# VectorE adds three of the last four pair sums of the softmax stage, and GpSimd does the small steps of the second norm's variances

## The chip, the cores and the metric

The kernel runs on one core of a Trainium2 chip. The metric is the device time of one execution in microseconds; the median of three runs is shown, with the lowest and the highest. The profile is of one more execution.

## What is computed

The input has four batches of 2048 tokens with 256 features. A block with two halves is applied to each batch. The first half is a layer norm with modulation, then attention by random features (16 heads, 64 features each). The second half is a second norm with modulation, a third norm, and softmax attention in which the tokens of expert e use only the first 256 / 2^e features.

```python
h = _layernorm(x, axis=-1) * (1 + ca) + sa
x = x + ga * _L0_attn_ref(h, ...)          # random features
h = _layernorm(x, axis=-1) * (1 + cb) + sb
x = x + gb * _L0_ffn_ref(h, ...)           # per token: xn = _layernorm(h), q, k, v by expert,
                                           # softmax(q k^T * scale) v over all 2048 tokens
```

A layer norm needs the mean and the variance of each token over its 256 features, and (variance + epsilon) to the power of -1/2.

## The kernel before, in words

Each engine has its own program, written out by hand, and semaphores tie them together. The loop over the four batches is written out too. A batch has three stages.

**First stage.** 16 tiles of 128 tokens: norm, projections, random features, sums over the keys. GpSimd prepares the first two tiles of the next batch in `begin` (two reciprocal roots L486, two normalised tiles `XH` L502), and `low_h` (L493) makes the low part `HTR` that TensorE's projection (L1424) needs.

**Middle stage.** The 2048 tokens are four slots of 512, and each slot has two halves (s, h) of two tiles. In the order of VectorE's program: `merged` (MT, L1147) multiplies numerators and reciprocals, TensorE projects (L1579), `residual` (L1154) adds, `statistics_of_x` takes the statistics of X (BATCH_NORM_STATS L1004, BATCH_NORM_AGGREGATE L1008 into MV, which holds mean and variance) and writes VE = variance + epsilon (L1014), GpSimd raises VE to -1/2 (RSTD, L572, in `deviations`), `modulated` (L1165, L1169) writes Hh, `statistics_of_h` takes the statistics of Hh and writes NEGM = -mean (L1013) and VE (L1014), and GpSimd writes RSTD (L577) and NMR = NEGM * RSTD (L579) in `deviations_again`. ScalarE then normalises (`centred`, L781, and `normal`, L793), TensorE makes queries and keys (L1608), ScalarE and VectorE write them as a high and a low part (QKS, L810 and L1179, `high_part` and `low_part`), and SyncE stores them and loads them back in the layout of the scores (the scratch tensors k_scr and q_scr, the tiles KOP and QOP). The interleaving of these steps is a list of calls in each engine's program. On GpSimd the list is `deviations(0, 0)`, `deviations(0, 1)`, `deviations_again(0, 0)` and so on.

**Softmax stage.** 64 steps called slots, in eight groups of eight (this slot is not the slot of 512 tokens). In each, TensorE makes four score tiles (L1705), ScalarE takes their exponentials into PR (L901), and TensorE multiplies by the values (L1717). The four tiles of a slot are added in pairs (the pair sum, TS0 and TS1) so that TensorE can form the denominators of two slots at once (L1730). GpSimd makes the pair sums (L631), except those of `VECTOR_SUMS`, slots 61 and 63 of 0 to 63, which VectorE makes (`pair_sum`, L1289). Beside this VectorE takes the maxima of scores of later units (L1111). In the last batches of slots GpSimd runs `begin(b + 1)` behind the sum of slot 60, and VectorE has begun the next batch just before its sum of slot 61. Behind slot 63 the order on TensorE is: the denominators of slots 62 and 63, the next batch's projection (L1424), its values (L1432), and the last output (L1785, L1787).

Of the kernel before, what the change touches and what calls it, by code (L numbers as in the profile page):

```python
# [7 lines left out]
ALU = mybir.AluOpType  # L8
# [12 lines left out]
NORM_EPS = 1e-5  # L21
# [24 lines left out]
def adaln_block(nc, x, Wq, Wk, Wv, Wo, bo, proj, norm_w, norm_b, q_w, q_b, k_w, k_b, v_w, v_b, o_w, o_b,  # L46
# [58 lines left out]
    with ExitStack() as ctx:  # L105
# [107 lines left out]
        def out_ps(e):  # L213
# [8 lines left out]
                   ve2 rs3 rstd2 ve3 nmr3 h2 x2 x2T xn_sb qp q_hi q_lo scr0 scr1 scr2 vp v2_sb vb_ok obm  # L222
# [85 lines left out]
        VECTOR_SUMS = (SLOTS - 3, SLOTS - 1)  # L308
# [163 lines left out]
        def _(pool):  # L472
            g = nc.gpsimd
# [68 lines left out]
            def batch(b):  # L542
# [26 lines left out]
                def deviations(s, h):  # L569
                    cols, n = halves(s, h), 2 * (NC * b + s) + h + 1  # L570
                    wait_all(pool, (S["ve2"], n))
                    g.tensor_tensor(RSTD[:, cols], VE[:, cols], minus_half[:, cols], ALU.pow).then_inc(S["rstd2"], 1)  # L572

                def deviations_again(s, h):
                    cols, n = halves(s, h), 2 * (NC * b + s) + h + 1
                    wait_all(pool, (S["ve3"], 2 * n))
                    g.tensor_tensor(RSTD[:, cols], VE[:, cols], minus_half[:, cols], ALU.pow).then_inc(S["rs3"], 1)  # L577
                    wait_all(pool, (S["rs3"], n))
                    g.tensor_tensor(NMR[:, cols], NEGM[:, cols], RSTD[:, cols], ALU.mult).then_inc(S["nmr3"], 1)  # L579
# [345 lines left out]
        def _(dve):  # L925
# [75 lines left out]
            def statistics(tiles, srcs, signal, negated=False):  # L1001
# [5 lines left out]
                for t in tiles:  # L1007
                    v.bn_aggr(MV[:, t], STAT[:, t]).then_inc(S["dve_own"], 1)  # L1008
                    own.n += 1
                dve.wait_ge(S["dve_own"], own.base + own.n)  # L1010
                sl = slice(tiles[0], tiles[-1] + 1)
                if negated:
                    v.tensor_scalar(NEGM[:, sl], MV[:, sl, 0], -1.0, None, ALU.mult).then_inc(S[signal], 1)  # L1013
                v.tensor_scalar(VE[:, sl], MV[:, sl, 1], NORM_EPS, None, ALU.add).then_inc(S[signal], 1)  # L1014
# [50 lines left out]
            def batch(b):  # L1065
# [106 lines left out]
                def statistics_of_h(s, h):  # L1172
                    dve.wait_ge(S["h2"], TPC * (NC * b + s) + 2 * h + 2)
                    statistics(halves(s, h), [Hh[:, t] for t in halves(s, h)], "ve3", negated=True)
# [72 lines left out]
                for m in range(SLOTS // 2):  # L1247
# [23 lines left out]
                    if 2 * m == SLOTS - 2:  # L1271
                        pair_sum(b, SLOTS - 1)
# [567 lines left out]
```

## Time and profile before

| what | value |
|---|---|
| median of three runs | 1766.48 us (1762.68 to 1766.83) |
| the profiled execution, its own time | 1768.27 us |
| its span, first to last instruction | 1766.5 us |
| mean granted TensorE clock | 0.974 |
| TensorE busy | 1678.5 us, 95% |
| VectorE busy | 1385.5 us, 78% |
| GpSimd busy | 1126.5 us, 64% |
| ScalarE busy | 1085.4 us, 61% |

The first batch ends at about 472 us of the span (the last addition into X, L1305, at 470.97), and each later one is some 431 us long, of which the middle stage has about 80 (165 to 245 us in the first batch) and the softmax stage about 220. In the timelines the columns are start, duration, engine, line, operation, output and input, how many are merged, and in brackets how long the engine had been idle and who released it. A busy TensorE is modelled, and the other engines' durations overlap a little between neighbours. Granted clock 1.00 is TensorE's upper level, 0.50 its lower.

### The profile page before, as it was taken

To read this page: it belongs to the slowest core of one execution; us is meant where nothing else is said; L and a number is where in the kernel's file an instruction comes from. 1 tells how busy PE (TensorE), PEld (TensorE's weight loads), DVE (VectorE), ACT (ScalarE), POOL (GpSimd) and SP (SyncE) were. 2 spreads that over 40 slices of the span, in tenths; PEclk is the share of its full clock that TensorE was granted. 3 is DMA by queue.
4 is the path that set the end of the run, shared out by engine and by line. 5 is a ranking of instruction groups with operands and counts; after the bars stand their busy time and mean duration, and the time that the engine had idled before them with its cause. 6 is when DMAs were issued, how large, how long until landed. Compare 5 with 4: busy or idle time off the path is not lost.

```text
span 1766.5 us, 32009 instructions
## 1 busy us (share of the span) xinstructions
PE 1678.5 (95%) x11538; PEld 970.8 (55%) x11538; DVE 1385.5 (78%) x2629; ACT 1085.4 (61%) x2066; POOL 1126.5 (64%) x1058
## 2 busy tenths in 40 slices
PE   6999989999999989999999998999999999899998
PEld 4776544444577554444467755444437765444443
DVE  5987978787688788787678878877858878787783
ACT  1885536566688553565668844466667875356665
POOL 2784358767678344867767734686686862477675
PEclk8999989999999998999999999999999999899999
DMA  6000360010200045001110005400120001520101
GB/s 188 2 1 1 103 188 15 19 46 25 73 2 1 1 152 143 10 19 46 58 40 2 2 16 174 106 19 10 46 72 25 2 1 58 179 61 18 39 17 48
DMA packets 56077, 89.57 MB, mean 51 GB/s; under 512 B 13288, under 2 KB 31976, under 8 KB 53100
## 3 DMA queue, kind: packets, MB, share of 16 engines
q1 hardware_dynamic: 54768, 87.45, 17.0%
q8 instruction: 93, 1.52, 0.4%
q14 instruction: 64, 0.52, 0.1%
q10 hardware_dynamic: 1152, 0.07, 0.0%
HBM read 49.29 MB, written 35.72 MB: 48 GB/s over the span
## 4 chain that ended last, share of the span: by engine, by line
PE 68%; DVE 16%; ACT 9%; DMA 2%; issue 2%; SPq 1%; POOL 1%; ACTq 0%; DVEq 0%; POOLq 0%
PE PS L1530 13%; PE PS L1705 12%; PE PS L1717 12%; PE PS L1730 6%; PE PS L1424 5%; DVE MXP L1111 4%; PE PS L1449 4%; PE PS L1432 3%; PE PS L1459 3%; ACT HT L670 2%; ACT HTR L673 2%; DVE STAT L1004 2%; ACT PR L901 2%; DVE QKS L1179 1%; ACT PHIQ L711 1%
## 5 line engine op out<-in xcount | busy, mean ns | idle before, releaser
L631 POOL TENSOR_TENSOR TS<-PR 128x1024 f32<-128x1024 f32 (+1 forms) x248 | 551.6, 2238 | 259.8 <-ACT PR L901 195.4
L1111 DVE TENSOR_REDUCE MXP<-PS 128x1 f32<-128x512 f32 x960 | 589.0, 681 | 145.9 <-PE PS L1530 145.2
L901 ACT ACTIVATE PR<-PS 128x512 f32<-128x512 f32 x960 | 487.6, 622 | 285.3 <-PE PS L1705 261.8
L1530 PE MATMUL PS<-KOP,QOP 96*128 96x512 f32 x960 | 406.8, 437 | 10.2 <-DVE MXP L1111 3.5
L1705 PE MATMUL PS<-QOP,KOP 97*128 97x512 f32 x960 | 376.5, 424 | 3.5 <-ACT QOP L888 3.1
L1530 PEld LDWEIGHTS PS<-KOP,QOP 96*128 96x128 f32 x960 | 186.2, 195 | 169.3 <-issue 90.4
L1705 PEld LDWEIGHTS PS<-QOP,KOP 97*128 97x128 f32 x960 | 180.3, 190 | 143.7 <-ACT PR L901 110.2
L1717 PE MATMUL PS<-PR,V 128*32 128x512 f32 x1920 | 255.1, 597 | 0.5
L1730 PE MATMUL PS<-TS,ones 128*32 128x512 f32 x960 | 136.0, 604 | 6.7 <-DVE TS L1289 6.7
L1717 PEld LDWEIGHTS PS<-PR,V 128*32 128x32 f32 x1920 | 62.2, 110 | 140.6 <-issue 98.4
L549 POOL TENSOR_SCALAR PK<-XSK 128x1024 f32<-128x1024 f32 x64 | 67.2, 1050 | 100.3 <-ACT XSK L733 100.3
L1459 PE MATMUL PS<-PB,QKT 64*128 64x256 f32 x1536 | 125.4, 296 | 1.0 <-DVE VE L998 1.0
L1459 PEld LDWEIGHTS PS<-PB,QKT 64*128 64x128 f32 x1536 | 99.2, 186 | 36.8 <-issue 24.4
L1424 PE MATMUL PS<-W1T,HTR 128*128 128x512 f32 x384 | 108.5, 419 | 3.7 <-POOL HTR L493 3.7
L509 POOL TENSOR_TENSOR SQ<-SQ 128x256 f32<-128x256 f32 (+2 forms) x192 | 95.9, 500 | 20.8 <-ACT SQ L690 6.0
L1051 DVE TENSOR_REDUCE MXQ<-PS 128x16 f32<-128x1024 f32 x64 | 78.4, 1224 | 21.8 <-PE PS L1459 21.2
L1449 PE MATMUL PS<-ident,XSQ 128*128 128x128 f32 x512 | 84.5, 292 | 9.8 <-ACT PHIQ L711 9.8
L502 POOL TENSOR_SCALAR XH<-X,MV,RSTD 128x256 f32<-128x256 f32 x64 | 78.7, 1229 | 11.0 <-POOL RSTD L486 10.4
L1061 DVE TENSOR_TENSOR XSK<-PS,MXK 128x1024 f32<-128x1024 f32 x64 | 78.4, 1225 | 7.1 <-DVE MXK L1057 0.9
L1051 DVE TENSOR_REDUCE MXK<-PS 128x16 f32<-128x1024 f32 x64 | 78.4, 1225 | 6.6 <-PE PS L1459 2.0
L711 ACT ACTIVATE PHIQ<-PS 128x512 f32<-128x512 f32 x128 | 76.5, 598 | 10.7 <-PE PS L1449 10.7
L1424 PEld LDWEIGHTS PS<-W1T,HTR 128*128 128x128 f32 x384 | 68.6, 192 | 25.1 <-POOL HTR L493 6.5
(157 smaller groups left out, 2524.1 us busy)
## 6 DMA issues: line engine op xcount, KB each, us to landing
KOP<-k_scr SPq DMA_DIRECT2D x84, 256.0 KB, 5.7
k_scr<-QKS SPq DMA_DIRECT2D x64, 256.0 KB, 2.9
QOP<-q_scr SPq DMA_DIRECT2D x180, 64.0 KB, 2.0
q_scr<-QKS SPq DMA_DIRECT2D x40, 256.0 KB, 3.0
X<-in_L_attn_x_dram SPq DMA_DIRECT2D x16, 512.0 KB, 3.9
out_dram<-X SPq DMA_DIRECT2D x12, 512.0 KB, 3.0
QOP<-MXT SPq DMA_DIRECT2D x224, 0.5 KB
KOP<-QKS SPq DMA_DIRECT2D x36, 64.0 KB, 2.0
```

What stands on the lines that cost most here:

```text
L509: g.tensor_tensor(sq[:, :, 0:w], sq[:, :, 0:w], sq[:, :, w:2 * w], ALU.add).then_inc(S["n2_half"], 1)
L631: g.tensor_tensor(sums(k)[:, 0:len(stage)], pair[:, :, 0], pair[:, :, 1], ALU.add).then_inc(S["psum_t"], 1)
L901: a.activation(PR[:, k % 2, w, q], bank(score_bank(p, n, w, q)), ACT.Exp).then_inc(S["ex"], 1)
L1051: return mark(v.tensor_reduce(mx[:], heads(src), AX.X, ALU.max))
L1111: v.tensor_reduce(MXP[:, u % 2, i, kc:kc + 1], bank(max_bank(p)), AX.X, ALU.max).then_inc(S["am_rd"], 1)
L1424: last = mm(bank(4), HTR[:, x_, k], W1T[:, w_, k], start=m == 0 and k == 0, stop=m == len(PARTS) - 1 and k == KD - 1)
L1449: last = tr(bank(at_bank)[:, q * P:(q + 1) * P], XSQ[:, t % 2, (half * 4 + q) * P:(half * 4 + q + 1) * P], ident[:])
L1459: last = mm(bank(base + r)[:, 2 * P * j:2 * P * (j + 1)], QKT[rows, x_, 2 * j + o], PB[rows, w_, j, 2 * P * r:2 * P * (r + 1)], start=m == ...
L1530: mm(bank(max_bank(p)), QOP[0:96, u % QS6, i * P:(i + 1) * P], KOP[0:96, h % KS6, kc * CH:(kc + 1) * CH], start=True, stop=True).then_inc( ...
L1705: mm(bank(score_bank(p, n, w, q)), KOP[:, units[u][0] % KS6, kt * P:(kt + 1) * P], QOP[:, u % QS6], start=True, stop=True).then_inc(S["sc_ ...
L1717: last = mm(PS[r:r + DH, 6, :], V2[:, 2 * n + q, h * DH:(h + 1) * DH], PR[:, k % 2, w, q], start=n == 0, stop=n == STEPS - 1, tile_positio ...
L1730: last = mm(PS[r:r + DH, 7, :], ones[:], sums(2 * m + q)[:, w], start=n == 0, stop=n == STEPS - 2, tile_position=(0, r))
```

## The change

Three edits. The sum of slot 62 joins `VECTOR_SUMS`, and VectorE makes it just before that of slot 63. `statistics` on VectorE ends with the aggregation, which signals by itself (one signal per tile, so the waits count two per half). VE and NEGM are now written by GpSimd, with three new semaphores between GpSimd's own steps.

```diff
-        VECTOR_SUMS = (SLOTS - 3, SLOTS - 1)
+        VECTOR_SUMS = (SLOTS - 3, SLOTS - 2, SLOTS - 1)
...
                 def deviations(s, h):
                     cols, n = halves(s, h), 2 * (NC * b + s) + h + 1
-                    wait_all(pool, (S["ve2"], n))
+                    wait_all(pool, (S["ve2"], 2 * n))
+                    g.tensor_scalar(VE[:, cols], MV[:, cols, 1], NORM_EPS, None, ALU.add).then_inc(S["ve2_e"], 1)
+                    wait_all(pool, (S["ve2_e"], n))
                     g.tensor_tensor(RSTD[:, cols], VE[:, cols], minus_half[:, cols], ALU.pow).then_inc(S["rstd2"], 1)
 
                 def deviations_again(s, h):
                     cols, n = halves(s, h), 2 * (NC * b + s) + h + 1
                     wait_all(pool, (S["ve3"], 2 * n))
+                    g.tensor_scalar(VE[:, cols], MV[:, cols, 1], NORM_EPS, None, ALU.add).then_inc(S["ve3_e"], 1)
+                    g.tensor_scalar(NEGM[:, cols], MV[:, cols, 0], -1.0, None, ALU.mult).then_inc(S["negm"], 1)
+                    wait_all(pool, (S["ve3_e"], n))
                     g.tensor_tensor(RSTD[:, cols], VE[:, cols], minus_half[:, cols], ALU.pow).then_inc(S["rs3"], 1)
-                    wait_all(pool, (S["rs3"], n))
+                    wait_all(pool, (S["rs3"], n), (S["negm"], n))
                     g.tensor_tensor(NMR[:, cols], NEGM[:, cols], RSTD[:, cols], ALU.mult).then_inc(S["nmr3"], 1)
...
-            def statistics(tiles, srcs, signal, negated=False):
+            def statistics(tiles, srcs, signal):
 
                 for t, src in zip(tiles, srcs):
                     v.bn_stats(STAT[:, t], src).then_inc(S["dve_own"], 1)
                     own.n += 1
                 wait_all(dve, (S["dve_own"], own.base + own.n))
                 for t in tiles:
-                    v.bn_aggr(MV[:, t], STAT[:, t]).then_inc(S["dve_own"], 1)
-                    own.n += 1
-                dve.wait_ge(S["dve_own"], own.base + own.n)
-                sl = slice(tiles[0], tiles[-1] + 1)
-                if negated:
-                    v.tensor_scalar(NEGM[:, sl], MV[:, sl, 0], -1.0, None, ALU.mult).then_inc(S[signal], 1)
-                v.tensor_scalar(VE[:, sl], MV[:, sl, 1], NORM_EPS, None, ALU.add).then_inc(S[signal], 1)
+                    v.bn_aggr(MV[:, t], STAT[:, t]).then_inc(S[signal], 1)
...
                         pair_sum(b, SLOTS - 3)
                     if 2 * m == SLOTS - 2:
+                        pair_sum(b, SLOTS - 2)
                         pair_sum(b, SLOTS - 1)
```

How the lists of instructions move is shown at three places. GpSimd, start of the middle stage of a batch, before (`PK`, `BOG` belong to the first stage):

```order
L540 TENSOR_TENSOR X<-X,BOG 128x256 x8
L572 TENSOR_TENSOR RSTD<-VE,minus_half 128x2 x2
L577 TENSOR_TENSOR RSTD<-VE,minus_half 128x2
L579 TENSOR_TENSOR NMR<-NEGM,RSTD 128x2
L577 TENSOR_TENSOR RSTD<-VE,minus_half 128x2
```

The same place in the changed program:

```order
L572 TENSOR_SCALAR VE<-MV 128x2 [waits ve2]
L574 TENSOR_TENSOR RSTD<-VE,minus_half 128x2 [waits ve2_e]
L572 TENSOR_SCALAR VE<-MV 128x2 [waits ve2]
L574 TENSOR_TENSOR RSTD<-VE,minus_half 128x2 [waits ve2_e]
L579 TENSOR_SCALAR VE<-MV 128x2 [waits ve3]
L580 TENSOR_SCALAR NEGM<-MV 128x2
L582 TENSOR_TENSOR RSTD<-VE,minus_half 128x2 [waits ve3_e]
L584 TENSOR_TENSOR NMR<-NEGM,RSTD 128x2 [waits negm,rs3]
```

GpSimd has one more step ahead of each first root and two ahead of each second one, and the root waits for GpSimd's own result.

VectorE at the same half as slot (1, 0), before:

```order
L1004 BN_STATS STAT<-X 128x6 x2
L1008 BN_AGGR MV<-STAT 128x2 x2
L1014 TENSOR_SCALAR VE<-MV 128x2
L1135 TENSOR_SCALAR R<-PS 128x4x8 x2
L1139 RECIPROCAL R<-R 128x64
L1165 SCALAR_TENSOR_TENSOR Hh<-X,MV,MODB 128x256 x2
```

and now, where the step on VE is gone and nothing else moved:

```order
L1009 BN_STATS STAT<-X 128x6 x2
L1013 BN_AGGR MV<-STAT 128x2 x2
L1134 TENSOR_SCALAR R<-PS 128x4x8 x2
L1138 RECIPROCAL R<-R 128x64
L1164 SCALAR_TENSOR_TENSOR Hh<-X,MV,MODB 128x256 x2
```

GpSimd at the end of a batch's softmax stage (the sum of slot 60, `begin` of the next batch, the sum of slot 62, `low_h`), before:

```order
L631 TENSOR_TENSOR TS0<-PR 128x1024
L486 TENSOR_TENSOR RSTD1<-VE1,minus_half 128x1
L502 TENSOR_SCALAR XH<-X,MV1,RSTD1 128x256
L486 TENSOR_TENSOR RSTD1<-VE1,minus_half 128x1
L502 TENSOR_SCALAR XH<-X,MV1,RSTD1 128x256
L631 TENSOR_TENSOR TS1<-PR 128x1024
L493 TENSOR_TENSOR HTR<-HT,HTR 128x256
```

and now, with the sum TS1 gone from between `begin` and `low_h`:

```order
L636 TENSOR_TENSOR TS0<-PR 128x1024
L486 TENSOR_TENSOR RSTD1<-VE1,minus_half 128x1
L502 TENSOR_SCALAR XH<-X,MV1,RSTD1 128x256
L486 TENSOR_TENSOR RSTD1<-VE1,minus_half 128x1
L502 TENSOR_SCALAR XH<-X,MV1,RSTD1 128x256
L493 TENSOR_TENSOR HTR<-HT,HTR 128x256
```

## Rows read from the trace of the kernel before

**Rows 1.** Busy time of each engine in one stretch of the middle stage, first batch (columns named there).

```profile
core 0: us, PE busy (x) PEld busy (x) DVE busy (x) ACT busy (x) POOL busy (x), PEclk, DMA share, GB/s
170.60:218.50 47.90, 46.76 (x240) 26.98 (x238) 46.50 (x149) 25.73 (x49) 13.35 (x24) 1.00 0.26 89
```

**Rows 2.** The pair-sum line L1289: durations of its eight, and who waited for it.

```profile
L1289 DVE TENSOR_TENSOR TS<-PR x8: 1539/1543/2965, 453.4 to 1752.9; 128x1024 f32<-128x1024 f32 x8
...
  PE PS L1730: 6.7, 4
```

**Rows 3.** VectorE in order of time: the last pair sum of batches one and four.

```profile
459.13 2.96 DVE L1289 TENSOR_TENSOR TS<-PR 128x1024 f32<-128x1024 f32 x1 [4.15 <-ACT PR L901]
...
1752.94 1.54 DVE L1289 TENSOR_TENSOR TS<-PR 128x1024 f32<-128x1024 f32 x1 [4.15 <-ACT PR L901]
```

**Rows 4.** ScalarE and GpSimd in the same order, end of batches one and four.

```profile
455.07 4.03 ACT L901 ACTIVATE PR<-PS 128x512 f32<-128x512 f32 x8 [1.67 <-PE PS L1705]
...
456.78 0.57 POOL L486 TENSOR_TENSOR RSTD<-VE,minus_half 128x1 f32<-128x1 f32 x1
457.46 1.23 POOL L502 TENSOR_SCALAR XH<-X,MV,RSTD 128x256 f32<-128x256 f32 x1
458.65 2.36 POOL L631 TENSOR_TENSOR TS<-PR 128x1024 f32<-128x1024 f32 x1
460.98 1.71 POOL L493 TENSOR_TENSOR HTR<-HT,HTR 128x256 fp32r<-128x256 f32 x1
...
1751.02 2.38 POOL L631 TENSOR_TENSOR TS<-PR 128x1024 f32<-128x1024 f32 x1 [3.32 <-ACT PR L901]
```

**Rows 5.** TensorE in order of time, end of batch one.

```profile
462.25 1.14 PE L1730 MATMUL PS<-TS,ones 128*32 128x512 f32 x8 [2.03 <-DVE TS L1289]
```

**Rows 6.** The stretch behind it by engine; the column after POOL is the granted clock.

```profile
464.00:466.00 2.00, 2.00 (x6) 1.58 (x5) 1.84 (x4) 0.02 (x1) 1.55 (x2) 0.50 0.03 8
```

**Rows 7.** VectorE in order of time, middle stage of batch one.

```profile
177.37 0.25 DVE L1008 BATCH_NORM_AGGREGATE MV<-STAT 128x2 f32<-128x6 f32 x2
...
177.80 0.88 DVE L1165 SCALAR_TENSOR_TENSOR Hh<-X,MV,MODB 128x256 f32<-128x256 f32 x2
...
182.70 0.25 DVE L1008 BATCH_NORM_AGGREGATE MV<-STAT 128x2 f32<-128x6 f32 x2
...
183.06 0.29 DVE L1135 TENSOR_SCALAR R<-PS 128x32 f32<-128x32 f32 x2
183.39 0.55 DVE L1139 RECIPROCAL R<-R 128x64 f32<-128x64 f32 x1
183.95 0.88 DVE L1165 SCALAR_TENSOR_TENSOR Hh<-X,MV,MODB 128x256 f32<-128x256 f32 x2
...
199.22 0.69 DVE L1147 TENSOR_TENSOR MT<-PS,NUMS 128x512 f32<-128x512 f32 x1
...
210.39 0.74 DVE L1179 SCALAR_TENSOR_TENSOR QKS<-PS,QBS,QKS 128x512 fp32r<-128x512 f32 x1
```

**Rows 8.** Groups of instructions by line (busy us, mean ns, idle before them).

```profile
L1579 PE MATMUL PS<-WoG,MT 128*128 128x256 f32 x256 | 59.5, 383 | 2.0 <-DVE MT L1147 2.0
...
L1008 DVE BATCH_NORM_AGGREGATE MV<-STAT 128x2 f32<-128x6 f32 x128 | 15.9, 166 | 2.2
```

**Rows 9.** GpSimd: line L579's durations; one reciprocal root in order of time.

```profile
L579 POOL TENSOR_TENSOR NMR<-NEGM,RSTD x32: 196/198/221, 178.9 to 1510.7; 128x2 f32<-128x2 f32 x32
...
183.23 0.69 POOL L572 TENSOR_TENSOR RSTD<-VE,minus_half 128x2 f32<-128x2 f32 x1 [0.90 <-DVE VE L1014]
```

**Rows 10.** ScalarE in order of time, middle stage of batch one.

```profile
198.53 0.60 ACT L762 ACTIVATE NUMS<-PS 128x512 f32<-128x512 f32 x1 [0.42 <-PE PS L1549]
...
209.32 0.68 ACT L810 ACTIVATE QKS<-PS,QBS 128x512 fp32r<-128x512 f32 x1
...
223.95 0.69 ACT L810 ACTIVATE QKS<-PS,QBS 128x512 fp32r<-128x512 f32 x1 [6.55 <-DMA k_scr<-QKS]
```

**Rows 11.** Durations of the modulation's first line, all batches.

```profile
L1165 DVE SCALAR_TENSOR_TENSOR Hh<-X,MV,MODB x64: 475/479/486, 174.4 to 1506.7; 128x256 f32<-128x256 f32 x64
```

More of the change, by code:

```diff
@@ L221, in adaln_block @@
                    den den_sb num num_sb denT rec rb rT mt yps x1
-                   ve2 rs3 rstd2 ve3 nmr3 h2 x2 x2T xn_sb qp q_hi q_lo scr0 scr1 scr2 vp v2_sb vb_ok obm
+                   ve2 ve2_e rs3 rstd2 ve3 ve3_e negm nmr3 h2 x2 x2T xn_sb qp q_hi q_lo scr0 scr1 scr2 vp v2_sb vb_ok obm
                    q_in0 q_in1 q_in2 q_in3 q_in4 q_in5 kf0 kf1 kf2 kf3 k_in1 k_in2 k_in3 k_in4 k_in5 k_in6 k_in7
@@ L1173, in statistics_of_h @@
                     dve.wait_ge(S["h2"], TPC * (NC * b + s) + 2 * h + 2)
-                    statistics(halves(s, h), [Hh[:, t] for t in halves(s, h)], "ve3", negated=True)
+                    statistics(halves(s, h), [Hh[:, t] for t in halves(s, h)], "ve3")
                 def low_part(s, i):
```

## The prediction

> **What bounds the kernel now.** I read the chain of waits first. Through most of the softmax stage it is TensorE, and there nothing that VectorE or GpSimd saves is worth anything. The two places of the change are exceptions, so I read each of them in its own rows.
>
> At the end of a batch TensorE stands idle for 2.03 us ahead of the denominators of the last two slots, and what it waits for is VectorE's sum of slot 63 [rows 5]. That line made TensorE wait four times, 6.7 us in all [rows 2]: once per batch, three like this and 6.7 - 3 x 2.03 = 0.6 us in the last batch. The sum took 2.96 us in batch one and 1.54 us in batch four, for the same work [rows 3]. The timelines say why. In batch four GpSimd's sum of slot 62 ended at 1751.02 + 2.38 = 1753.40 and VectorE's at 1752.94 + 1.54 = 1754.48, 1.08 us later. In batch one GpSimd ended at 458.65 + 2.36 = 461.01 and VectorE at 462.09, again 1.08 us later [rows 3, 4]. So the two engines do not overlap in such additions: the sum itself takes 1.08 us, and the rest is standing behind GpSimd, which in batches one to three starts its sum late, behind `begin`.
>
> In the middle stage both engines are nearly full: of 47.90 us VectorE is busy 46.50 and TensorE 46.76 [rows 1]. VectorE's program runs there without gaps, and the chain of waits goes through it from 170.6 us to the `low_part` at 210.39 [rows 7]. From that one it goes through SyncE's stores and loads to ScalarE at 223.95, which had waited 6.55 us for a store to land [rows 10]. An earlier `low_part` therefore moves all of this, and with it the start of the softmax stage.
>
> **Part one, the sum of slot 62.** The exponentials of slot 62 are the first four of the eight from 455.07 (4.03 us), so they are there at about 457.1 [rows 4]. GpSimd is then in its second root, until 456.78 + 0.57 = 457.35. VectorE's sum of slot 62 would run from 457.35 to 458.43, and GpSimd's second XH (1.23 us) behind it to 459.66. Slot 63 is ready at 459.1, and its sum runs from 459.66 to 460.74. TensorE takes it up 0.16 us later (462.09 to 462.25 before), at 460.90 instead of 462.25: a gain of 1.35 us in each of three batches. If XH is first, the sums end at 459.77 and 460.85, and the gain is 1.24. TensorE's next work also needs HTR: it ended at 460.98 + 1.71 = 462.69 with VectorE in its way, and now waits only until 460.74 and ends by 461.5, while the denominators last to about 462.0. So nothing takes the place of the wait. In batch four there is no `begin`: the sum of slot 63 starts at 1752.94 as before and takes 1.08 instead of 1.54 us, a gain of 0.46. What GpSimd no longer does (four sums of 2.37 us) is worth nothing by itself, since it has nothing late behind it. **Together 3 x 1.35 + 0.46 = 4.5 us.** The bounds are 4.2 (XH first each time) and 6.7, the whole wait.
>
> The Trainium skill ("SBUF — State Buffer", Who interferes with whom) has a rule for what these rows show: an instruction of VectorE with two SBUF inputs and one of GpSimd that reads SBUF exclude each other, and the second "fully blocks" until the first is done. By it the new sum of slot 62 blocks GpSimd's XH as worked out, so rule and rows give the same here. They part in the middle stage, below.
>
> A second effect: behind the 2.03 us of idleness the granted clock is 0.50, the lower level of 1.2 GHz, for a few us in batch one [rows 6]. With 0.6 to 0.7 us of idleness, as in batch four, it may stay at 2.4 GHz. That would be up to another 1.3 us once. The middle stage has such stretches too, and they may shift either way, so I put the clock at nothing and keep 2 us for the range.
>
> **Part two, the small steps.** VectorE loses 64 steps on VE and 32 on NEGM. What a removed step is worth is the time until the next one starts. The second of two aggregations starts 0.25 - 0.166 = 0.084 us after the first, so the next independent instruction could start 0.17 us after the first [rows 7, 8]. Now it starts 183.06 - 182.70 = 0.36 us after it for X and 177.80 - 177.37 = 0.43 us for Hh: gains of 0.19 and 0.26 us. Up to `low_part` at 210.39 there are eight halves of X and six of Hh: 8 x 0.19 + 6 x 0.26 = **3.1 us** per batch that VectorE could be earlier there. Two things eat of it.
>
> First, GpSimd's new steps stand ahead of the roots. No row shows this add. The nearest is L579, also 128x2 on GpSimd, with 0.198 us; the farthest is XH, the same operation, but 128x256 with two scalars read from memory, with 1.23 us [rows 4, 9]. I take 0.20. `modulated(1, 0)` is where it bites: its root ran from 183.23 to 183.92 and VectorE took it at 183.95 [rows 7, 9], so the root was already as late as VectorE itself. With 0.08 us for a signal, the chain is now aggregation's end + 0.08 + 0.20 + 0.08 + 0.69 + 0.03 = 1.08 us, instead of 1.00. VectorE stands there about 0.25 us, and at `modulated(1, 1)`, where GpSimd first has the four steps of the half before, about as long again. Some 0.5 us are lost.
>
> Second, TensorE. `merged` at 199.22 needs NUMS, which ScalarE ended at 198.53 + 0.60 = 199.13, out of TensorE [rows 7, 10]. TensorE had only one wait for VectorE before it, L1579, 2.0 us in four batches, 0.5 us each [rows 8]. So at 199.22 VectorE is only about 0.5 us earlier, whatever it saved. Behind it are X (2,1), Hh (2,0), Hh (2,1), X (3,0), X (3,1): 3 x 0.19 + 2 x 0.26 = 1.1 us more, less what ScalarE's part holds back: its QKS started at 209.32 and ended at 210.00, 0.39 us ahead of VectorE's, and goes by NMR, which comes 0.5 + 0.45 - 0.15 = 0.8 us earlier. So `low_part` can come 0.8 + 0.39 = **about 1.1 us** earlier. Four batches give 4.4 us. The bounds are 4 x 3.1 = 12.4 and, if GpSimd's step costs what XH does, a loss (second rival).
>
> **The sum** is 4.5 + 4.4 = 8.9 us. From the profiled execution's own 1768.27 that is 1759.4. It lies 1.8 us above the median of the runs, so the median would be **1757.6 us**, 0.5% less. Some 0.3% (5.3 us) is what a measurement can tell from no change.
>
> **Rivals.**
> *Only the end of the batch gains.* TensorE has 1.1 us of idleness in those 47.90 [rows 1], and if it and SyncE's queue, not VectorE, set the start of the softmax stage, part two gives 0 to 0.3 us per batch: 1766.48 - 4.5 - 0.6 = 1761.4. For it: TensorE's busy time. Against it: the gapless VectorE, and the store that waits for its `low_part`. Chance 0.2.
>
> *GpSimd's steps are dear; slower than before.* It is decided at `modulated(1, 1)`. GpSimd has three of the new steps between the aggregation of Hh (1, 0) and the root that VectorE needs there. With c for each, that root is ready 3 x (c - 0.2) later than worked out above. VectorE is then some 0.7 us ahead of before, so part two is at zero from c = 0.2 + 0.7 / 3 = 0.43 us on. At XH's 1.23 us it loses 3 x 1.03 - 0.7 = 2.4 us there, and as much again in later halves, where three to four such steps stand between roots: 4 x 4.8 = 19 us, less 4.5, gives 1781. It ends over 0.3% slower (5.3 us) from 2 x (3 x (c - 0.2) - 0.7) = (5.3 + 4.5) / 4 on, which is c = 0.84 us. For it: XH is the same operation. Against it: XH's 1.23 us is for 256 columns, and L579 with the same two columns takes 0.198. Chance 0.04.
>
> *The ports give it back.* L1165 and L1169 on VectorE have two SBUF inputs, and 24 more GpSimd instructions per batch fall among them. If each held VectorE up for its own 0.2 us, that is 4.8 us per batch against 8 x 0.19 + 8 x 0.26 = 3.6 saved: part two loses 4 x 1.2 = 4.8 us, and the whole stands at 1766.8, no change. Against it: GpSimd's roots already fall among these 64 instructions, and L1165 took 475 to 486 ns each time, never longer [rows 11]. Chance 0.07. The Trainium skill's rule (same page and section) would bring this about, and speaks against the change. By that rule, a few rows of L1165 should be longer, and none is.
>
> *Everything and the clock.* The lower clock at the batch's end goes and TensorE's small waits in the middle stage close: part two gives 2 us per batch, 1766.48 - 4.5 - 8 - 1.3 = 1752.7. Chance 0.12.
>
> The forecast itself has 0.57. That the change doesn't do what it says is ruled out by the lists of instructions.
>
> **How the numbers follow.** The forecast's own range is 1757.6 with 3 us for the clock and the runs' scatter: 1754.5 to 1760.5. The range takes in most of the first and the last rival: 1752.0 to 1762.5. It leaves out the slower case and the ports. Faster by over 0.3% is below 1761.2: nearly all of the forecast (0.55), the last rival (0.12), and near half of the first (0.09): 0.76. Within 0.3%: the rest of the first (0.11), of the forecast (0.02) and the ports (0.07), 0.20. Slower: 0.04.
>
> **What would show it.** Right, if the eight pair sums of VectorE become twelve of 1.1 to 1.6 us with none of 2.96, TensorE's wait for them falls from 6.7 us to under 3, the first batch ends 2 to 4 us earlier, GpSimd's new instructions take about 0.2 us, and `low_part` comes near 209.3 instead of 210.39. Wrong, if the new steps take over 0.4 us, if VectorE shows waits for RSTD of over 0.5 us per half, if L1165 gets longer, or if `low_part` is earlier but ScalarE's 223.95 is not.

## The result, and the profile after

| what | before | after |
|---|---|---|
| median of four runs each | 1766.65 us (1762.68 to 1767.3) | **1751.39 us** (1751.28 to 1752.34) |
| the profiled execution, its own time | 1768.27 us | 1751.49 us |
| its span | 1766.5 us | 1749.7 us |
| mean granted clock | 0.974 | 0.98 |

The ratio is 0.9915 with a 95% interval of 0.9901 to 0.9928: faster by 15.3 us, where 8.9 had been forecast. The sign and both mechanisms held. The size did not, and the time lies below the whole range. Later measurements of the kernel before, each with more runs, gave 1765.0 to 1766.7 us, so the gain is 13.6 to 15.3 us.

The end of batch one first. The views are those of [rows 2 to 5]: the pair-sum line, then VectorE, GpSimd and TensorE in order of time.

```profile
L1289 DVE TENSOR_TENSOR TS<-PR x12: 1224/1226/1550, 451.9 to 1737.8; 128x1024 f32<-128x1024 f32 x12
...
  PE PS L1730: 1.1, 4
```

```profile
451.89 1.54 DVE L1289 TENSOR_TENSOR TS<-PR 128x1024 f32<-128x1024 f32 x1 [3.39 <-ACT PR L906]
455.62 1.22 DVE L1289 TENSOR_TENSOR TS<-PR 128x1024 f32<-128x1024 f32 x1 [2.19 <-ACT PR L906]
457.58 1.23 DVE L1289 TENSOR_TENSOR TS<-PR 128x1024 f32<-128x1024 f32 x1 [0.74 <-ACT PR L906]
```

```profile
449.98 2.37 POOL L636 TENSOR_TENSOR TS<-PR 128x1024 f32<-128x1024 f32 x1 [1.40 <-ACT PR L906]
...
455.23 0.57 POOL L486 TENSOR_TENSOR RSTD<-VE,minus_half 128x1 f32<-128x1 f32 x1
455.91 2.04 POOL L502 TENSOR_SCALAR XH<-X,MV,RSTD 128x256 f32<-128x256 f32 x1
459.07 0.73 POOL L493 TENSOR_TENSOR HTR<-HT,HTR 128x256 fp32r<-128x256 f32 x1 [1.12 <-ACT HTR L678]
```

```profile
458.96 1.07 PE L1730 MATMUL PS<-TS,ones 128*32 128x512 f32 x8 [0.29 <-DVE TS L1289]
```

The sum of 2.96 us is gone. TensorE's wait is 0.29 us instead of 2.03 [rows 5], and 1.1 us over the four batches instead of 6.7 [rows 2].

The middle stage, with the stretch of [rows 1] at the same place, and then GpSimd's new steps by line (columns: shortest, median and longest in ns), its roots and who waited for them, and the modulation's first line.

```profile
170.88:218.78 47.90, 47.33 (x244) 27.67 (x242) 45.42 (x128) 25.69 (x49) 20.96 (x50) 1.00 0.29 94
```

```profile
L572 POOL TENSOR_SCALAR VE<-MV x32: 215/224/361, 172.8 to 1488.2; 128x2 f32<-128x2 f32 x32
...
L580 POOL TENSOR_SCALAR NEGM<-MV x32: 222/230/328, 178.0 to 1494.9; 128x2 f32<-128x2 f32 x32
...
L574 POOL TENSOR_TENSOR RSTD<-VE,minus_half x32: 699/704/807, 173.1 to 1488.5; 128x2 f32<-128x2 f32 x32
...
  DVE Hh L1164: 3.6, 8
...
L1164 DVE SCALAR_TENSOR_TENSOR Hh<-X,MV,MODB x64: 451/478/486, 174.3 to 1491.7; 128x256 f32<-128x256 f32 x64
```

VectorE has 21 instructions less there and TensorE is at 47.33 of 47.90 us. A new step costs 0.22 us, and VectorE now waits twice in each batch for a root, 3.6 us in all. In order of time VectorE's waits behind its roots and behind ScalarE in batch one are these, followed by its `low_part`:

```profile
183.74 0.88 DVE L1164 SCALAR_TENSOR_TENSOR Hh<-X,MV,MODB 128x256 f32<-128x256 f32 x2 [0.37 <-POOL RSTD L574]
...
189.63 0.88 DVE L1164 SCALAR_TENSOR_TENSOR Hh<-X,MV,MODB 128x256 f32<-128x256 f32 x2 [0.52 <-POOL RSTD L574]
...
206.49 0.75 DVE L1178 SCALAR_TENSOR_TENSOR QKS<-PS,COLS,QKS 128x512 fp32r<-128x512 f32 x1 [0.45 <-ACT QKS L815]
...
209.07 0.75 DVE L1178 SCALAR_TENSOR_TENSOR QKS<-PS,QBS,QKS 128x512 fp32r<-128x512 f32 x1
```

TensorE at `projected`, before and after (L1579 had its wait of [rows 8]), and ScalarE after:

```profile
188.88 0.60 PE L1557 MATMUL PS<-ident,DENS 128*128 128x128 f32 x4
189.99 1.97 PE L1579 MATMUL PS<-WoG,MT 128*128 128x256 f32 x8 [0.51 <-DVE MT L1147]
```

```profile
188.97 0.60 PE L1557 MATMUL PS<-ident,DENS 128*128 128x128 f32 x4
189.41 1.89 PE L1579 MATMUL PS<-WoG,MT 128*128 128x256 f32 x8
```

```profile
L1579 PE MATMUL PS<-WoG,MT 128*128 128x256 f32 x256 | 59.3, 382 | 0.0
```

```profile
205.77 0.69 ACT L815 ACTIVATE QKS<-PS,COLS 128x512 fp32r<-128x512 f32 x1 [0.93 <-PE PS L1608]
206.47 1.09 ACT L786 ACTIVATE X<-Hh,NMR,RSTD 128x256 f32<-128x256 f32 x2
...
208.37 0.67 ACT L815 ACTIVATE QKS<-PS,QBS 128x512 fp32r<-128x512 f32 x1
...
222.65 0.69 ACT L815 ACTIVATE QKS<-PS,QBS 128x512 fp32r<-128x512 f32 x1 [6.12 <-DMA k_scr<-QKS]
```

I measure the middle stage from its first addition into X (170.64 us before, 170.92 after) to this `low_part` (210.39 before, 209.07 after). This stretch was 39.75 us in batch one and 39.73 in the others, and is 38.15 in all four now: **1.6 us per batch, 6.3 in all**, where I had 1.1 and 4.4. ScalarE's 223.95 [rows 10] came to 222.65, so the gain passes through SyncE's stores. Not all of it reaches the scores, as the sum below shows.

The two parts give 5.5 us (TensorE's waits of 6.7 and 1.1 us [rows 2]) and 6.3 us, together 11.8. The span fell by 16.8. Most of what is left is TensorE's clock. Four windows before and the same four after: the first stage of batches two and three (from the last addition into X of one batch to the copy of DENS in the next), and the stretch from the last denominators to the last addition into X in batches one and two. The first number behind the window is its length; the granted clock stands behind POOL.

```profile
472.25:589.32 117.07, 109.95 (x1241) 86.32 (x1240) 103.15 (x150) 96.32 (x177) 85.13 (x131) 0.99 0.03 11
902.16:1019.36 117.20, 110.22 (x1241) 86.32 (x1240) 103.32 (x152) 96.26 (x177) 85.20 (x131) 0.99 0.04 11
...
462.25:472.25 10.00, 10.00 (x52) 7.44 (x52) 6.89 (x16) 4.10 (x9) 4.47 (x8) 0.83 0.01 2
893.71:902.16 8.45, 8.45 (x52) 6.33 (x52) 7.26 (x16) 4.10 (x9) 4.48 (x8) 1.00 0.01 2
```

```profile
467.47:583.22 115.75, 108.86 (x1243) 85.78 (x1240) 102.75 (x151) 96.16 (x177) 83.97 (x130) 1.00 0.04 11
894.26:1010.28 116.02, 109.22 (x1243) 85.76 (x1240) 103.10 (x152) 96.00 (x177) 83.97 (x130) 1.00 0.04 11
...
458.96:467.47 8.51, 8.51 (x52) 6.36 (x52) 7.47 (x16) 4.67 (x10) 5.07 (x8) 1.00 0.01 2
885.74:894.26 8.52, 8.52 (x52) 6.36 (x52) 7.47 (x16) 4.68 (x10) 5.07 (x8) 1.00 0.01 2
```

The same 52 matmuls take 10.00 us at a mean granted clock of 0.83 and 8.5 at 1.00. A first stage is 117.1 us with 3.3 us at the lower level (0.50, that is 1.2 GHz) and 115.8 to 116.0 with at most 0.2. In all, 92.2 us of the span of before were at the lower level and 71.7 of this one. By stretches the 16.8 us are: middle stage 6.3, softmax stage from first scores to last addition into X 8.0 (5.5 by the wait, 2.5 by the clock: a low stretch less in batch one and one less in batch four), later first stages 3.9 by the clock, and 1.6 us lost just ahead of the first scores. Of these, 1.2 us are in batch two, where TensorE stood 2.29 us for a load into KOP after the change and 0.34 before it; that is no loss by the clock.

The low time of a first stage lies at its end, where TensorE waits for GpSimd's PK in both kernels and equally long:

```profile
587.32 1.08 PE L1475 MATMUL PS<-PK,V 128*32 128x128 f32 x16 [2.97 <-POOL PK L549]
```

```profile
582.07 0.64 PE L1475 MATMUL PS<-PK,V 128*32 128x128 f32 x16 [2.94 <-POOL PK L549]
```

Before, the low level began at 585.98 us, inside that wait, and L1475 and what follows it ran slowly. After, it began at 583.46, behind the start of those matmuls. So this part of the gain does not come from a shorter idleness at this place: the low level came at another moment of the same work.

### The profile page after: what moved, and what is told of

Read it like the earlier page. It is cut to its first block, busy times and chain, and to the rows that moved or that the text cites. A ratio compares the mean times of both kernels' runs of the same rounds, so it can differ in the third digit from the quotient of the medians.

```text
span 1749.7 us, 32041 instructions
## 1 busy us (share of the span) xinstructions
PE 1669.2 (95%) x11538; PEld 966.2 (55%) x11538; DVE 1371.5 (78%) x2537; ACT 1085.2 (62%) x2066; POOL 1140.7 (65%) x1150
## 4 chain that ended last, share of the span: by engine, by line
PE 75%; DVE 10%; ACT 9%; DMA 2%; issue 1%; SPq 1%; POOL 1%; ACTq 0%; DVEq 0%; POOLq 0%
PE PS L1530 13%; PE PS L1705 12%; PE PS L1717 12%; PE PS L1730 6%; PE PS L1424 5%; DVE MXP L1110 4%; PE PS L1449 4%; PE PS L1432 3%; PE PS L1459 3%; PE PS L1579 3%; ACT HT L675 3%; ACT HTR L678 2%; ACT PR L906 2%; PE PS L1540 2%; PE PS L1549 2%
## 5 line engine op out<-in xcount | busy, mean ns | idle before, releaser
L636 POOL TENSOR_TENSOR TS<-PR 128x1024 f32<-128x1024 f32 (+1 forms) x244 | 541.9, 2234 | 258.4 <-ACT PR L906 193.1
```

Source lines behind the costliest of these rows:

```text
L636: g.tensor_tensor(sums(k)[:, 0:len(stage)], pair[:, :, 0], pair[:, :, 1], ALU.add).then_inc(S["psum_t"], 1)
```

## The experiments

Each program's profile (one execution of each) was cut into the same stretches; "low" is the time at the lower clock level within one. Times are medians with the lowest and highest; "its before" is the kernel before measured in the same comparison (1766.69 us for the first four, 1764.95 to 1765.27 for the others).

### Each part alone

**Only part one**: `VECTOR_SUMS` and the added `pair_sum(b, SLOTS - 2)`, nothing else.

> Part one alone: slot 62's sum goes to VectorE, the small steps stay. Both theories: TensorE's wait for the pair sums falls from 6.7 to about 1.2 us, 5.5 us less. Theory A (the clock's stretches moved): the first stage, from the last addition into X to the copy of DENS, takes 117.1 or 115.8 us depending on how long the clock is low in it, so the whole gains 5.5 us plus 0 to 6, and the two parts measured alone need not add up to 15.2. Theory B (part one itself shortens the next batch's first stage by 1.3 us): the first stage takes 115.8 us in batches two to four here, and the whole gains 5.5 + 3.9 = 9.4 us or slightly more.

**Only part two**: the steps on VE and NEGM to GpSimd, the sums as before.

> Part two alone: VE and NEGM on GpSimd, the pair sums as before. Both theories: from the first addition into X to low_part of query block five 38.15 us instead of 39.73, 1.6 us per batch, 6.3 us. Theory A: the whole gains 6.3 us plus or minus up to 5 by the clock. Theory B: the first stage stays at 117.1 us, and the whole gains 6 us, so that the parts' gains add up to 15.2.

**Only X's step, or only those of Hh**:

```diff
-                    wait_all(pool, (S["ve2"], n))
+                    wait_all(pool, (S["ve2"], 2 * n))
+                    g.tensor_scalar(VE[:, cols], MV[:, cols, 1], NORM_EPS, None, ALU.add).then_inc(S["ve2_e"], 1)
+                    wait_all(pool, (S["ve2_e"], n))
```

> Part two for X's statistics alone (VE of the first root on GpSimd), Hh's steps stay on VectorE. By the record's steps (0.19 us each) eight of X are worth up to 1.5 us per batch less the waits for the root. By the theory that TensorE's start of the projection (L1579, slot two) limits it: first addition to low_part about 0.8 us shorter. By the rival that the gain is VectorE's freed time only: 1.1 to 1.5 us.

> Part two for Hh's statistics alone (VE and NEGM of the second root on GpSimd), X's step stays on VectorE. Six of Hh are worth up to 1.6 us per batch. If TensorE's start of L1579 limits it, the stretch from the first addition to low_part gets about 1.0 us shorter; if only freed time counts, 1.6 us. Its gain and that of the X part should add up to less than 1.6 us plus the waits for roots that both share (0.9 us).

| kernel | time | ratio to its before | middle stretch | first stages 2, 3, 4 (low) |
|---|---|---|---|---|
| part one | 1757.56 (1754.61 to 1760.8) | 0.9941 [0.9923, 0.9959] | 39.73 | 116.7 (2.9), 115.9 (0.2), 116.9 (3.0) |
| part two | 1760.85 (1758.04 to 1763.53) | 0.9968 [0.9955, 0.998] | 38.16 | 115.9 (0), 117.0 (3.3), 116.6 (2.5) |
| X alone | 1760.31 (1759.29 to 1760.79) | 0.9961 [0.9946, 0.9976] | 38.63 | 116.6 (2.6), 116.9 (3.1), 116.9 (2.7) |
| Hh alone | 1764.19 (1762.32 to 1768.1) | 0.9987 [0.9978, 0.9997] | 38.64 | 117.2 (3.2), 115.9 (0), 116.6 (3.1) |

The parts gain 9.1 and 5.8 us, together 15.0 of the 15.3. These times alone are what theory B gave (9.4 and 6), so they do not decide between the two. The stretches do: part two takes 1.6 us from the middle stretch, X or Hh alone 1.1 each, and together not 2.2 but 1.6, so something else takes over as the bound. Part one leaves it at 39.73. X alone and Hh alone have the same middle stretch and yet differ by 3.9 us: Hh alone had 10.0 us behind the last denominators in all of batches one to three, X alone in none. A first stage follows its own time at the low clock in every kernel, whichever part it has. Theory B wanted 115.8 us in all three batches of part one alone, and two of them are 116.7 and 116.9 us. That speaks for theory A.

### What bounds the middle stage now

**Two calls of GpSimd's list exchanged** in the changed kernel:

```diff
-                deviations_again(1, 0)
                 deviations(1, 1)
+                deviations_again(1, 0)
```

> The changed kernel with two neighbouring calls of GpSimd's list exchanged: deviations(1, 1) ahead of deviations_again(1, 0). The root that VectorE waits 0.52 us for at modulated(1, 1) then comes without the four steps ahead of it, and that wait goes (to under 0.1 us). Theory T (once VectorE has lost its steps, TensorE with L1579 and ScalarE behind it set low_part, not VectorE's waits for roots): the stretch from the first addition into X to the low_part of block 5 stays at 38.15 us, within 0.1. Rival V (what I put on record: VectorE's waits at modulated(1,0) and (1,1) take part of the gain): the stretch gets 0.4 to 0.5 us shorter, to about 37.7, and the time 1.6 to 2 us. Time by T 1751.4, give or take 3 for the clock; by V 1749.5, give or take 3.

1751.29 us (1749.71 to 1756.3), and the middle stretch is 38.15 us in all four batches. The same modulation and `low_part` in VectorE's timeline of this kernel, whose middle stage began 0.98 us earlier:

```profile
188.04 0.87 DVE L1164 SCALAR_TENSOR_TENSOR Hh<-X,MV,MODB 128x256 f32<-128x256 f32 x2
...
208.09 0.75 DVE L1178 SCALAR_TENSOR_TENSOR QKS<-PS,QBS,QKS 128x512 fp32r<-128x512 f32 x1
```

The wait of 0.52 us is gone and nothing is gained by it: 208.09 + 0.98 = 209.07, as before the exchange. Theory T is right to the hundredth, and the wait taken away was not on the path. The other one, 0.37 us at `modulated(1, 0)`, is still there and was not tested by itself. The path runs through L1579, the next products, ScalarE's QKS at 205.77 and `centred` at 206.47.

**GpSimd's new steps done twice** (the extra results go into tiles that nobody reads; shown for the second root, and the first root's step on VE is doubled in the same way):

```diff
+                    g.tensor_scalar(EX1[:, cols], MV[:, cols, 1], NORM_EPS, None, ALU.add).then_inc(S["ve3_e"], 1)
                     g.tensor_scalar(VE[:, cols], MV[:, cols, 1], NORM_EPS, None, ALU.add).then_inc(S["ve3_e"], 1)
+                    g.tensor_scalar(EX2[:, cols], MV[:, cols, 0], -1.0, None, ALU.mult).then_inc(S["negm"], 1)
```

> The changed kernel with each of GpSimd's new steps done twice, the extra ones into tiles that nobody reads: c goes from 0.22 to about 0.44 us per step, 64 + 32 steps more. What I put on record for the rival of dear steps: from c = 0.43 on part two is worth nothing, since the root of modulated(1, 1) comes 3 x 0.22 = 0.66 us later; then the stretch from the first addition into X to the low_part of block 5 would be 39.7 us again, and the time about 1751.4 + 6.3 = 1757.7. Theory T (only halves where VectorE already waits for its root pass the delay on, and TensorE and ScalarE set the end): VectorE's wait at (1,1) grows by about 0.7 us, half or more of it reaches low_part, the stretch is 38.3 to 38.9 us and the time 1752 to 1754.5, give or take 3 for the clock.

1757.17 us (1755.81 to 1759.0), middle stretch 39.29: longer by 1.14 us, between the two theories (39.7 and at most 38.9), with a time near the rival's 1757.7. GpSimd's last NMR ahead of `low_part` and ScalarE say why; first that NMR in the changed kernel, then the rows of this one.

```profile
206.24 0.20 POOL L584 TENSOR_TENSOR NMR<-NEGM,RSTD 128x2 f32<-128x2 f32 x1
```

```profile
206.52 0.19 POOL L588 TENSOR_TENSOR NMR<-NEGM,RSTD 128x2 f32<-128x2 f32 x1
```

```profile
206.75 1.09 ACT L790 ACTIVATE X<-Hh,NMR,RSTD 128x256 f32<-128x256 f32 x2 [0.83 <-POOL NMR L588]
...
208.64 0.68 ACT L819 ACTIVATE QKS<-PS,QBS 128x512 fp32r<-128x512 f32 x1
```

That NMR began 35.32 us into the stretch in the changed kernel and 36.46 here (206.52 - 170.06), 1.14 later, and the whole of it reached the end. In the changed kernel ScalarE finished QKS at 206.46 and NMR was there at 206.44: two chains, TensorE's and GpSimd's, arrived within 0.02 us of each other. So theory T held towards faster steps and not towards slower ones; and at c = 0.44 us part two still gained 0.44 us per batch, where my rival of dear steps had it at zero from 0.43 on.

### How much of the gain is the clock

**Pads.** In the kernel before and in the changed one, TensorE's four small products ahead of the first scores are made once, twice or three times more, 0.88 us each:

```diff
-                for i in range(TPC):
+                for i in list(range(TPC)) * 2:
                     last = mm(PS[96:97, 7, i * P:(i + 1) * P], MXN[:, 0, i:i + 1], ident[:], start=True, stop=True,
```

> The kernel before, with one run of TensorE matmuls per batch made twice (the work on L1737, once more over the same tiles: about 0.9 us per batch at the upper clock), and nothing else. Rival (the clock plays no part in the 15 us; the rest of the gain came out of the two parts in a way not found yet): 1766.7 + 4 x 0.9 = 1770.3, and the three later first stages (last addition into X of one batch to the first addition into X of the next) longer or equal, 117.1 to 118.1 us, never shorter. Theory A (a small shift in time moves the stretches of low clock, and each one in a first stage costs about 1.2 us): the time lies up to 4 us off 1770.3 on either side, at least one of the three first stages has no time at the low clock and comes out 1 us shorter than its neighbours, and the middle stretch stays 39.73 us in every batch, since VectorE and GpSimd have nothing changed.

> As the kernel with one pad, with two of them (about 1.8 us per batch). Rival (no clock): 1766.7 + 4 x 1.8 = 1773.9 and a straight line through before, one pad and two pads within 1 us. Theory A: off that line by up to 4 us, with the total time at the low clock in the profile higher where the time is above the line and lower where it is below, about 0.4 us of time for 1 us at low clock; middle stretch 39.73 us.

> The kernel before with three pads (3 x 0.88 us of TensorE per batch, between the middle stage and the first scores). It is one of a row of kernels that shift everything behind by 0.88 us per pad and batch, to see how the time of the same work scatters: 1766.7 + 10.6 = 1777.3 with no clock in it. With the clock (theory A): up to 5 us off on either side, the middle stretch 39.73 us.

> The changed kernel with one pad. Theory L (luck of the phase: what the change gives by itself is 5.5 + 6.3 = 11.8 us, and the clock adds or takes up to 5 as the shift falls): the gain against the kernel before with the same pad is different from 15.2, somewhere from 7 to 17, and the mean over none, one, two and three pads comes near 12. Theory S (the changed kernel keeps TensorE's clock up as such, since its idle stretches are shorter): the gain is 14 to 17 us with every number of pads, that is 1775.1 - 15.2 = 1759.9 here, and the total time at the low clock is some 20 us less than in the partner each time. The middle stretch is 38.15 us in both.

> The changed kernel with two pads, against the kernel before with two pads (1774.8). Theory S: 1774.8 - 15.2 = 1759.6. Theory L: 1751.4 + 7 = 1758.4 shifted by up to 5 us either way, so the gain is anything from 8 to 20 and its mean over the four pairs near 12. Total at low clock and time go together in both.

> The changed kernel with three pads, against the kernel before with three pads on the same chip. Theory S: 14 to 17 us less than it. Theory L: 7 to 17 us less, with the mean over the four pairs near 12. In either, first stages without time at the low clock are 115.8 to 116.1 us and those with 2.5 us or more of it 116.6 to 117.2.

| pads | before | low, all | changed | low, all | difference |
|---|---|---|---|---|---|
| 0 | 1766.65 | 92.2 | 1751.39 | 71.7 | 15.3 |
| 1 | 1775.09 (1770.41 to 1776.91) | 99.0 | 1755.7 (1753.69 to 1756.03) | 71.7 | 19.4 |
| 2 | 1774.81 (1773.07 to 1776.13) | 95.6 | 1760.51 (1757.65 to 1762.76) | 75.1 | 14.3 |
| 3 | 1773.58 (1772.71 to 1774.8) | 75.9 | 1762.11 (1758.19 to 1764.75) | 71.7 | 11.5 |

The kernel before is no straight line. With 3.5 us more work per row its time rises by 8.4 us, then falls by 0.3 and by 1.2, and three pads are faster than one; the middle stretch is 39.7 us in each. One pad lies 4.8 us above the line and has 6.8 us more low time than none, three pads lie 3.6 us below it and have 16.3 us less. So the rival without a clock is out. The difference goes from 11.5 to 19.4 us with a mean of 15.1. S (14 to 17 each time) is out. L wanted 7 to 17 each time and a mean near 12: one value lies above, and the mean of 15.1 is uncertain by some 2 us with four such values, so 12 is not excluded by the times. Taken as they are, about 3.3 us (15.1 - 11.8) come with the change on the mean, and up to 4 either way are the phase, that is, which work the low clock happens to fall on. (With the 1765 us that later comparisons gave for the kernel before, the first row would be 13.6 and the mean 14.7.) The profiled executions, one of each kernel, differ by 16.6 us on the mean of the four rows: middle stage 6.3, first scores to last addition 9.0 (5.5 of it the wait), later first stages 2.3, lost elsewhere 1.0. The first stages had more than 1 us at the low clock in 10 of 12 batches of the kernel before and in 3 of 12 of the changed one. The other kernels of this text make that weaker: it was 5 of 12 in the four others that have the whole change (calls exchanged, steps doubled, late by one and by two sums), 9 of 12 in the four with one part or a piece of it, and 5 of 6 in the two filled ones.

### What the shorter idleness does

Up to here the fourteen profiles (the text below says eleven) showed a pattern in batches one to three. Behind an idleness of 2.03 us ahead of the last denominators the stretch to the last addition into X was 10.0 us in 10 of 21 batches; behind 0.3 us it was 8.5 us in 21 of 21. Each profile is one execution, so these are counts over kernels and batches, not over repeated runs. Four more kernels test it. **Fill**: the kernel before, and that with one pad, get useless work in the idle time.

```diff
+                if following is not None:
+                    for _ in range(5):
+                        mm(bank(score_bank(...)), KOP[...], QOP[...], start=True, stop=True)
                 denominators(SLOTS // 2 - 1)
```

> The kernel before, in which TensorE fills its 2.03 us of idleness ahead of the last denominators of batches one to three with work that nobody needs: the last score product five more times (5 x 0.35 us) into a bank that is free by then. Over the eleven profiles so far the stretch from these denominators to the last addition into X was 10.0 us (3.4 us of it at the low clock) in 10 of 21 batches behind an idleness of 2.03 us, and 8.5 us in 21 of 21 behind 0.3 us. Theory I (the length of the idleness decides): 8.5 us here in all three batches, 1.5 us less than before in one of them, so the time is 1765 although it does 15 products more. Rival R (only the phase decides, and the change had luck): about half of the batches of this kernel and the two below stay at 10.0 us.

> The same filling in the kernel before with one pad, where all three batches had 10.0 us there (time 1775.1). Theory I: 8.5 us in all three, so 4.6 us less, 1770.5, if the rest keeps its phase; rival R: 10.0 us in one or more of them and 1775.

**Late**: the changed kernel makes slot 62's sum twice or three times in batches one to three.

```diff
+                if k == SLOTS - 2 and b < B - 1:
+                    for _ in range(2):
+                        own(v.tensor_tensor(sums(k), pair[:, :, 0], pair[:, :, 1], ALU.add))
                 v.tensor_tensor(sums(k), pair[:, :, 0], pair[:, :, 1], ALU.add).then_inc(S["psum_v"], 1)
```

> The changed kernel in which VectorE makes the sum of slot 62 twice in batches one to three, each waiting for the one before: TensorE's idleness ahead of the last denominators goes from 0.3 to about 1.5 us. Direct cost 3 x 1.2 = 3.7 us, that is 1755.1. Theory I: if 1.5 us is enough, some of the three stretches are 10.0 us and the time 1.5 more for each; if not, all stay at 8.5. Rival R: all 8.5 or any.

> The same with the sum of slot 62 made three times: idleness about 2.7 us, direct cost 3 x 2.44 = 7.3 us, that is 1758.7. Theory I: the low clock is back behind it in one to three batches (10.0 us), so 1760 to 1763, and the changed kernel has lost its gain of the clock there. Rival R: the stretches stay at 8.5 us as in the changed kernel, 1758.7, give or take 3.

| kernel | time | idle ahead of the last denominators | to the last addition, batches 1, 2, 3 |
|---|---|---|---|
| before | 1766.65 | 2.03 | 10.00, 8.45, 8.45 |
| before, filled | 1764.9 (1762.9 to 1766.81) | 0.68 | 8.45, 8.45, 8.45 |
| one pad | 1775.09 | 2.02 | 10.04, 10.04, 10.05 |
| one pad, filled | 1768.35 (1767.71 to 1770.26) | 0.68 | 8.46, 8.46, 8.45 |
| changed | 1751.39 | 0.29 | 8.51, 8.52, 8.52 |
| changed, late by one sum | 1753.14 (1752.88 to 1754.7) | 0.96 | 8.47, 8.46, 8.45 |
| changed, late by two sums | 1760.61 (1757.69 to 1761.81) | 2.75 | 8.47, 9.96, 9.97 |

The stretches of batch one with one pad, then the same filled, then all three of the changed kernel late by two sums:

```profile
463.76:473.80 10.04, 10.04 (x52) 7.50 (x52) 7.42 (x16) 4.09 (x9) 4.33 (x8) 0.83 0.01 2
```

```profile
462.26:470.72 8.46, 8.46 (x52) 6.33 (x52) 7.26 (x16) 4.09 (x9) 4.49 (x8) 1.00 0.01 2
```

```profile
460.32:468.79 8.47, 8.47 (x52) 6.33 (x52) 7.26 (x16) 4.09 (x9) 4.04 (x7) 1.00 0.01 2
889.45:899.41 9.96, 9.96 (x52) 6.87 (x52) 7.70 (x16) 4.09 (x9) 4.14 (x7) 0.84 0.01 2
1319.52:1329.49 9.97, 9.97 (x52) 6.87 (x52) 7.70 (x16) 4.09 (x9) 4.14 (x7) 0.83 0.00 0
```

Theory I fits all of it, and rival R, which wanted about half of the filled batches at 10.0 us, does not. Behind 2.0 to 2.8 us of idleness the low clock came in 12 of 24 batches, behind 0.3 to 1.0 us in none of 30. The kernel late by one sum reached 0.96 us of idleness instead of the 1.5 expected, so nothing between 1.0 and 2.0 us was measured. With fifteen products more, the filled kernel with one pad is 6.7 us faster than the same without them; 4.8 us of that is this stretch (30.13 - 25.37), and the rest fell elsewhere. Filling the unpadded kernel takes 1.5 us from this stretch in the profiled execution and shows nothing in the time (0.9997 [0.9988, 1.0007]). Why is not shown: the 10.0 us may be missing in many executions of the unfilled kernel too, or other stretches may have given it back. A long idleness is thus needed here and not enough by itself: X alone had 2 us of it and no low clock. Batch four, where other work follows, is different: there 3.4 us at the low clock fell between the last denominators and the last addition in four of the nine profiles with 0.60 us of idleness, and in none of the nine with 0.29. It began 5.5 us behind the denominators' start, where TensorE has stood idle for another 0.36 and 1.44 us. So the rule is told for batches one to three only.

## Why the prediction was right and wrong

- **Part one's mechanism**: right. No sum of 2.96 us is left, HTR (0.73 us, ended at 459.80) holds nobody up, and nothing took the wait's place.
- **Part one's size, 3 x 1.35 + 0.46 = 4.5 us**: mis-sized. It measured 3 x (2.03 - 0.29) + (0.60 - 0.29) = 5.5 us. Two steps failed, one by 0.53 us and one by 0.14 the other way, and 1.35 + 0.53 - 0.14 is the 1.74 measured. "The sum itself takes 1.08 us" was what is left of it once GpSimd is out of the way; with no GpSimd instruction beside it, in batch four, it takes 1.22. And I had the sum of slot 62 wait for GpSimd's root until 457.35 and push the XH behind it, so that slot 63's began late. In fact it started at 455.62, while the root ran (455.23, 0.57 us), took its 1.22 us, and the XH behind it took 2.04 instead of 1.23. Slot 63's sum then found VectorE free and waited only for its data. The "no overlap" that I had read between two large additions does not hold for a root of one column. By the rule that the prediction cites from the Trainium skill ("SBUF — State Buffer", Who interferes with whom), the sum of two SBUF inputs should have stood until the root was done at 455.80; the trace decides against it here, as far as GpSimd's recorded spans, which are rough, can be trusted to 0.2 us. The other order did show blocking: a root issued at 452.30, behind a sum begun at 451.89, took 1.55 us.
- **Part two's mechanism**: right, and the new step's cost too (0.22 for 0.20). The waits at `modulated(1, 0)` and `(1, 1)` came where I had put them, 0.37 and 0.52 us for 0.25 each, but the step that counted 0.5 us as lost is wrong at least for the second: with that one taken away nothing moved.
- **Part two's size, 4.4 us**: 6.3. The step that failed is "at 199.22 VectorE is only about 0.5 us earlier", out of L1579's wait of 0.51 us. Measured from the first addition into X, L1579 began 0.86 us earlier (189.99 - 189.41 + 0.28). A recorded wait counts from the modelled end of the matmuls before (188.88 + 0.60), and after shows the next ones 0.44 us behind their start: 0.16 us of the idleness was hidden in that. The rest is that L1557 itself came 0.19 us earlier in the stretch. The same 0.4 us appears behind it: NMR, which I had 0.8 us earlier, came 1.23 us earlier (207.19 - 206.24 + 0.28), and with the 0.39 us that `low_part` had stood behind ScalarE's QKS this is the 1.6 measured. The sum had a slip too: 0.8 + 0.39 is 1.2, not 1.1, which would have made 4.8 us of the 4.4.
- **The clock at nothing, with 2 us for the range**: the largest miss, and the step that put the time out of the range. In the two executions shown the clock gave 2.5 + 3.9 = 6.4 us, and 16.8 - 11.8 = 5 us were left of it; on the mean over four shifts it was 3.3 us, uncertain by some 2. How much fell to these two kernels is in part luck of the phase. My "up to 1.3 us once" was right in kind (1.5 us), but it is at stake in each of three batches, not in one. Batch four, which I had taken as free of it, had a low stretch too: 9.13 us from its last denominators to the last addition before, 7.78 after. The first stages were not looked at.
- **The rivals.** Only the end of the batch gains: out, 222.65 instead of 223.95. Dear steps: out, at 0.22 us. The ports give it back: out; L1164 takes 451 to 486 ns, no longer than before [rows 11]. By the Trainium skill's rule ("SBUF — State Buffer", Who interferes with whom) some should be longer: of the 128 instructions of the modulation, 56 started while a GpSimd instruction still had 0.13 to 0.66 us to run, and these took 476 to 484 ns. What grew instead, up to 0.36 us for 0.22, was a GpSimd step behind VectorE. "Everything and the clock", 1752.7, was nearest, and I had given it 0.12.
- **The range** ended at 1752.0, 0.6 us above the result. With the clock's phase alone worth 4 us either way, as the pads show, it had to be wider by about that.

## What to carry to other kernels

When TensorE drives a kernel, read the granted clock by stretches in both traces before you credit a gain to the edit: cut the program into the same stretches and compare only those, since a shift of a few us moved the whole by up to 5 us here. Price a removed wait by when the thing waited for will be ready, not by the wait's recorded length: behind matmuls, whose ends are modelled, a wait of 0.51 us stood for 0.67 here. An idleness of 2 us in front of dense TensorE work can cost more than its own length. Filling it with useless work gained 6.7 us in one kernel here and nothing in another, so it is worth a try beside the edit that removes the cause.

## What the runs showed of the hardware

- Ahead of the last denominators of batches one to three the low clock followed a long idleness only sometimes: in 12 of 24 batches behind 2.0 to 2.8 us, in none of 30 behind up to 1.0 us. Where it came, 3.4 us at the low level cost 1.5 us of time. Why the later first stages had more than 1 us of it in 8 batches of 24 in the kernels with the whole change, against 24 of 30 in the others, was not found and stays open; the wait of about 3 us at their end is in both, and the pads were not run with one part alone.
- VectorE's addition of two 128x1024 tiles takes 1.22 us. It took no longer where it started while a one-column root was running on GpSimd (0.57 us), and the GpSimd instruction behind it took 2.04 us for 1.23. GpSimd's own addition of that size takes 2.37 us, so VectorE is the faster engine for it by almost two.
- GpSimd's steps on two columns took 0.22 us, and up to 0.36 (0.43 where doubled) behind a VectorE instruction with two SBUF inputs; that instruction of VectorE, the modulation's first line, never got longer:

```profile
201.80 0.36 POOL L579 TENSOR_SCALAR VE<-MV 128x2 f32<-128x2 f32 x1 [0.51 <-DVE MV L1013]
202.24 0.32 POOL L580 TENSOR_SCALAR NEGM<-MV 128x2 f32<-128x2 f32 x1
```
